# Graph attention with a mixture of experts on one core: reordered normalisation, scanned bf16 ranks, a bf16 table of slots ahead of the shared outputs, and a fourth buffer for edge keys

## The chip, the cores and the metric

The kernel runs on 1 core of one Trainium2 chip. The metric is the device time of one execution in microseconds (us); lower is better. A core has five engines with queues of their own: PE (TensorE, matmuls), DVE (VectorE), ACT (ScalarE), POOL (GpSimd, which here gathers and scatters rows by indirect DMA) and SP (SyncE, which issues most transfers). They meet only at semaphores: `wait_ge` holds up the engine's whole queue, `then_inc` signals at the end of an instruction.

## The reference, cut to what matters

1250 tokens of 512 numbers, 20000 edges sorted by destination, 64 experts.

```
x = x + gnn(layernorm(x))                 # graph attention, 8 heads of 64
   h = x @ W.T;  e = leaky_relu(e_src[src] + e_dst[dst]) * (1 + et_emb[type]) * weight
   alpha = softmax of e over the edges of one dst
   out = layernorm(sum over edges of h[src] * alpha + x) * ln_gamma + ln_beta
x = x + ffn(layernorm(x))
   scores = sigmoid(x @ Wg.T + bg);  w, idx = top 2 of 64, w normalised
   y = sum over the two experts of w * (silu(h1) * h3) @ W2 + b2   # own gamma, beta, W1, W3 per expert
   z = shared expert: (silu(nxs @ Ws1 + bs1) * (nxs @ Ws3 + bs3)) @ Ws2 + bs2
   result x + y + z
```

## The kernel before

All numbers of the tokens live in SBUF as NT = 10 tiles of 128 rows. The program is written out by hand, one block for each engine, and the order of each queue is the order of the code. Its stages, in order of time:

**Selection of attention terms.** Per edge and head, `e_src[src]` and `e_dst[dst]` are picked by matmuls with one-hot matrices. The keys (src mod 128, dst mod 128, type) lie in DRAM as `edge_keys`. 160 chunks of 128 edges make 16 pieces of 10 chunks, each read in two groups of 5 (32 groups). For a piece SP loads three key rows, broadcast over the partitions, into one of three buffers (`keys[q % 3]`, L414); it waits until PE has done piece q-3. DVE makes one-hots of src and type (`hot`, L1241 and L1243), ACT those of dst (`hot_dst`, L659 and L661), PE multiplies (L920, L925), DVE picks (L1340) and sums (L1289). Both `hot(q + 2)` and `hot_dst(q + 2)` stand in their queues ahead of the last group of piece q. After each odd group up to 19 PE also computes one tile of h (L901), ACT copies it out and SP stores it (`HELD`, L419) behind the keys of piece t+3. Once all ten are stored, POOL starts its 176 gathers of h rows (L569).

**Softmax and items.** DVE scans, then 88 items of two gathered chunks each are scaled by DVE and ACT, summed by PE (L969) and added by DVE (L1445). POOL's gathers reuse 23 pairs of buffers, so gather 46 waits for the first item.

**Normalisation and router.** The tiles go in five steps of two (`LNG`). DVE: `gnn_sum` (statistics, L1491 and L1494), `x1_sum` (L1505 to L1515), `x1_scale` (L1520 to L1522, which waits for ACT's square roots), `best_two` (logits and top 2, L1529 to L1537). ACT: `root` (L715), `x1_spread` (L721 to L725), `x1_normalise` (L731, and L735, the copies of the transposed tiles). PE: four transposes a tile (L825) and four logit matmuls (L994). The order of DVE is

```
                if 0 <= step - 2 < G:
                    x1_scale(step - 2)
                if step < G:
                    gnn_sum(step)
                if 0 <= step - 1 < G:
                    x1_sum(step - 1)
```

**Ranks and slots.** From the top 2 DVE makes one-hots over experts (`oh`), their sum `hits`, and the running sum over tiles `before` (ten dependent adds, L1597). PE turns these into ranks within each expert by matmuls with a triangle and with ones (f32, L1030 to L1032). A chain of some 25 DVE instructions (L1601 to L1633) makes the slot of each token. Then `rank1h` (L1637) and `tile1h` (L1639, times `payload` L1641) are multiplied on PE (20 f32 matmuls of 72 columns, L1042) into the table of slots, of which DVE makes indices (L1648 to L1652) and POOL the first two gathers of tokens (L594).

**Shared expert beside it.** `shared_up(k)` (L1008) is two halves of four f32 matmuls of 512 columns each (gate and up), `shared_gate` its silu on ACT (L753), `shared_hidden` the product on DVE (L1549); `shared_down(t)` (L1014) and `shared_add` (L1542) give tile t. `sil` is one buffer, so gate k waits for hidden k-1. PE's order is up(0), ranks, up(1), up(2), down(0), down(1), table of slots, up(3), turn of the first tokens, down(2), then the pair loop, in which the rest of the shared work is spread by `BESIDE` (`aside`).

**Pair loop.** 32 pairs of experts and one overflow expert, NJ = 33 steps. Step j: `up` (L1071, L1075), the turn of the next tokens (L825), `down` of step j-1 (L1088), `aside(j)`, `hidden_turn`. Weights lie in three buffers; SP loads the 2 MB of up weights of step j+3 when PE has done up of step j (L445), ACT the 1 MB of down weights after `down` (L777). At the end POOL has scattered the expert rows to `y_rows`, and SP, DVE and ACT bring them back, add and store them tile by tile.

## Time and profile before

| what | us |
|---|---|
| median of 3 runs (lowest, highest) | 751.66 (750.05, 753.65) |
| the profiled execution | 749.77 |
| its span | 748.0 |
| busy in the span: PE, DVE, ACT, POOL | 612.7, 486.6, 234.5, 263.0 |

The profiled execution's time is 1.8 us above its span; the span is what the engines' rows cover, and all rows shown here count from its start. The stages lie about like this in it: selection 42 to 149, softmax 149 to 181, items 181 to 356, normalisation and router 356 to 405, ranks and slots with the first shared work 405 to 448, pair loop 448 to 718, the end to 748. A stretch's row gives each engine's busy time with the number of instructions, then the clock granted to PE as a share of 2.4 GHz, the busy share of the DMA engines and what they moved.

### The profile page before, as it was taken

The page shows a single profiled execution, that of the slowest core. Times are in us where ns is not written, and L with a number is a line of the kernel's source. Part 1 is how long each engine was busy: PE and PEld are TensorE (multiplying, and loading weights), DVE is VectorE, ACT ScalarE, POOL GpSimd, SP SyncE. Part 2 cuts the span into 40 slices and gives each one's busy share as a digit, 9 for nine tenths or more (in the row PEclk, how much of TensorE's full clock was granted, in tenths as well). Part 3 has the DMA queues.
Part 4 walks back from the last instruction along what each step waited for, and adds up shares of the span by engine and source line. Part 5 has one row for each costly group of instructions (what it writes and reads, how often), then busy time and mean ns, then how long its engine had stood idle before and what let it go on. Part 6 is the DMA issues. An engine that isn't in the chain of part 4 may idle for free. (4 is left out here: it accounts for less than half of the span.)

```text
span 748.0 us, 9448 instructions
## 1 busy us (share of the span) xinstructions
PE 612.7 (82%) x3091; PEld 297.1 (40%) x3091; DVE 486.6 (65%) x950; ACT 234.5 (31%) x575; POOL 263.0 (35%) x281
## 2 busy tenths in 40 slices
PE   2979996534999999999089999999999999998940
PEld 2645665522333333333077453443333333332310
DVE  5886778897999999998777745533233333332307
ACT  1563554514755443435276210111111111111110
POOL 3000005775777777778400011222222222222210
PEclk9898998655999999999655999999999999998985
DMA  8433667866779977795721007999999999999929
GB/s 258 122 82 100 158 157 240 252 182 174 209 211 336 361 227 211 212 371 177 273 85 56 1 19 276 397 379 409 414 414 412 409 414 411 380 379 414 364 79 364
DMA packets 68135, 194.30 MB, mean 260 GB/s; under 512 B 14539, under 2 KB 15621, under 8 KB 68086
## 3 DMA queue, kind: packets, MB, share of 16 engines
q1 hardware_dynamic: 37270, 100.70, 37.2%
q0 software_dynamic: 19600, 56.41, 23.9%
q10 hardware_dynamic: 11216, 36.58, 12.6%
q8 instruction: 25, 0.41, 0.2%
q14 instruction: 24, 0.20, 0.1%
HBM read 184.31 MB, written 16.58 MB: 269 GB/s over the span
## 5 line engine op out<-in xcount | busy, mean ns | idle before, releaser
L599 POOL DMA_INDIRECT y_rows<-nxb,slot_tab x33 | 34.3, 1040 | 193.1 <-ACT nxb L784 191.2
L1711 DVE TENSOR_TENSOR nxb<-ps,nxb 128x256 f32<-128x256 f32 (+1 forms) x33 | 14.0, 424 | 134.3 <-PE ps L1075 73.1
L569 POOL DMA_INDIRECT nxb<-h_rows,srcx x50 | 47.5, 951 | 128.8 <-DMA h_rows<-ring 108.9
L1075 PE MATMUL ps<-arena,nxb 128*64 128x512 f32 x352 | 82.1, 609 | 0.0
L569 POOL DMA_INDIRECT ring<-h_rows,srcx x74 | 71.0, 960 | 23.5 <-issue 20.7
L969 PE MATMUL ps<-ring,edge 128*128 128x512 f32 x148 | 67.3, 603 | 7.4 <-issue 6.8
L825 PE MATMUL ps<-ident,nxb 128*128 128x128 f32 (+1 forms) x248 | 49.5, 321 | 20.3 <-ACT nxb L731 19.7
L825 PEld LDWEIGHTS ps<-ident,nxb 128*128 128x128 f32 (+1 forms) x248 | 39.2, 207 | 65.2 <-issue 57.7
L1088 PE MATMUL ps<-arena,nxb 128*64 128x512 f32 x260 | 63.9, 604 | 0.9 <-DVE nxb L1714 0.9
L1445 DVE TENSOR_TENSOR xn<-ps,xn 128x512 f32 x88 | 60.9, 692 | 2.4 <-PE ps L969 1.5
L781 ACT ACTIVATE nxb<-ps 128x256 f32<-128x256 f32 (+1 forms) x33 | 12.7, 384 | 155.5 <-PE ps L1075 155.5
L707 ACT ACTIVATE ring<-ring,edge 128x64 f32<-128x64 f32 x148 | 37.7, 335 | 58.0 <-DVEq L1434 39.5
L969 PE MATMUL ps<-nxb,edge 128*128 128x512 f32 x100 | 46.4, 615 | 6.0 <-ACT nxb L707 4.2
L784 ACT COPY nxb<-ps 128x512 f32<-128x512 f32 (+1 forms) x33 | 19.3, 585 | 83.4 <-PE ps L1088 83.4
L969 PEld LDWEIGHTS ps<-ring,edge 128*128 128x128 f32 x148 | 26.2, 189 | 47.4 <-issue 47.4
L1340 DVE TENSOR_TENSOR x_sb<-ps,arena 128x400 f32<-128x400 f32 x64 | 33.5, 562 | 17.4 <-PE ps L925 16.5
L569 POOL DMA_INDIRECT xT<-h_rows,srcx x42 | 40.1, 954 | 12.8 <-issue 11.3
L1075 PE MATMUL ps<-edge,nxb 128*64 128x512 f32 x168 | 42.8, 632 | 0.0
L901 PE MATMUL ps<-arena,xT 128*128 128x512 f32 x80 | 40.0, 645 | 3.4 <-DVE dloc L1281 3.4
L594 POOL DMA_INDIRECT nxb<-nx_rows,slot_tab x34 | 34.7, 1020 | 20.2 <-issue 10.7
L1075 PEld LDWEIGHTS ps<-arena,nxb 128*64 128x64 f32 x352 | 23.7, 138 | 45.3 <-issue 45.3
L969 PE MATMUL ps<-xT,edge 128*128 128x512 f32 x84 | 37.9, 601 | 2.1 <-issue 1.8
(300 smaller groups left out, 1047.0 us busy)
## 6 DMA issues: line engine op xcount, KB each, us to landing
arena<-in_L_ffn_W_dram SPq DMA_DIRECT2D x47, 1024.0 KB, 12.4
arena<-in_L_ffn_W_dram ACTq DMA_DIRECT2D x29, 1024.0 KB, 10.4
edge<-in_L_ffn_W_dram SPq DMA_DIRECT2D x20, 1024.0 KB, 12.6
arena<-edge_keys SPq DMA_DIRECT2D x22, 320.0 KB
ring<-y_rows SPq DMA_DIRECT2D x9, 512.0 KB, 6.9
ring<-edge_keys SPq DMA_DIRECT2D x10, 320.0 KB
h_rows<-ring SPq DMA_DIRECT2D x10, 256.0 KB, 2.0
nx_rows<-nxb SPq DMA_DIRECT2D x10, 256.0 KB, 2.0
```

What stands on the lines that cost most here:

```text
L569: pool.indirect_dma_start(out=slot(k), out_offset=None, in_=h_d[:, :], in_offset=bass.IndirectOffsetOnAxis(ap=srcx[:, k:k + 1], axis=0)).t ...
L594: pool.indirect_dma_start(out=xg[:, u, :], out_offset=None, in_=nx_d[:, :], in_offset=bass.IndirectOffsetOnAxis(ap=at, axis=0), bounds_che ...
L599: pool.indirect_dma_start(out=y_d[:, :], out_offset=bass.IndirectOffsetOnAxis(ap=at, axis=0), in_=yo[:, u, :], in_offset=None, bounds_chec ...
L707: o = act.activation(slot(k)[:, h * HD:(h + 1) * HD], slot(k)[:, h * HD:(h + 1) * HD], ACT.Copy, scale=p_c[:, k, h:h + 1])
L784: act.copy(yo[0:rows, k, :], ps[0:rows, 5 + k, :]).then_inc(s(done), 1)
L825: return pe.transpose(o, i, ident[0:n, 0:n])
L901: o = pe.matmul(ps[:, 7, :], xT[:, a, t * P:(t + 1) * P], WT[:, a, :], start=(a == 0), stop=(a == A - 1))
L969: o = pe.matmul(ps[:, BANKS[i % len(BANKS)], :], S[:, k % (2 * SB), :], slot(k), start=(u == 0), stop=(u == 1))
L1075: o = pe.matmul(ps[c, 2 + k, :], xgT[:, k, a, c], w13[b][:, x, :, a, :], start=False, stop=(a == A - 1), skip_group_check=True)
L1088: o = pe.matmul(ps[c, 5 + k, :], hT[:, k, m, c], w2s[b][:, x, m, :], start=(m == 0), stop=(m == M - 1))
L1340: v.tensor_tensor(pr[:, side, :, :, :], ps[:, 2 * (g % 2) + side, 0:n * NT * H].rearrange("p (c h a) -> p c h a", c=n, a=NT), sel_hi[:, si ...
L1445: v.tensor_tensor(a, ps[:, BANKS[i % len(BANKS)], :], a, ALU.add).then_inc(s("acc_done"), 1)
```

## The change

1. **Fourth key buffer.** `keys` gets a fourth buffer in tiles 4 to 7 of `x_sb`, free once the first layer norm is done; `% 3` becomes `% 4`, SP waits for piece q-4, and the stores of h stand behind the keys of piece t+4, with the same waits in front of them.
2. **Order of normalisation.** On DVE `gnn_sum(step)` comes ahead of `x1_scale(step - 2)`. `rank_masks` (casts of the triangle and of ones, and two memsets) is added ahead of `bias_high`.
3. **Ranks.** `hits` is written expert-major in bf16; one scan over 640 elements, reset at every expert by a mask, replaces the ten adds; the rank matmuls are bf16 (480 and 160 columns) and come after only the first half of up(0).
4. **Slots.** The one-hots are bf16. The payload is split: position and side within a tile, which bf16 holds exactly, in `tile_lo` on DVE, and 256 t in `tile_hi`, nine small activations on ACT. 20 + 18 bf16 matmuls sum both in one bank. They come ahead of down(0) and down(1). DVE runs `shared_hidden(0)` after the chain of slots and `shared_hidden(1)` after the one-hots.
5. **Banks and order of the shared work.** up(k) gets banks of its own in PSUM with fewer waits; only half of up(3) stays ahead of the loop, the other half goes into step 0 (`BESIDE`).

```diff
@@ keys and their loads
+        keys.append(Carver(x_sb[:, 4:8, :].rearrange("p t d -> p (t d)"), 4 * D)([P, 3, PIECE * P], BF16))
-            HELD[min(GROUPS[g][0] + 3, len(PIECES) - 1)].append(t)
+            HELD[min(GROUPS[g][0] + 4, len(PIECES) - 1)].append(t)
-                if q >= 3:
-                    sp.wait_ge(s("pe_sel"), sum(1 for g in GROUPS if g[0] <= q - 3))
+                if q == 3:
+                    sp.wait_ge(s("ln1"), NT)
+                if q >= 4:
+                    sp.wait_ge(s("pe_sel"), sum(1 for g in GROUPS if g[0] <= q - 4))
...
@@ banks and spread of the shared work
+    BESIDE = {0: (("half", 3),), 2: (("up", 4),), ...
+    UP_BANKS = ((4, 5), (1, 2), (4, 5), (3, 5), (1, 7), (1, 7))
+    UP_FREE = ((0, 0), (0, 0), (1, 1), (0, 3), (4, 4), (5, 5))
...
@@ ACT, ahead of gates 2 and 3
+                    if n == 1:
+                        act.wait_ge(s("route_step"), 2)
+                        for t in range(1, NT):
+                            o = act.activation(tile_hi[:, 2 * t:2 * t + 2, :], tile1h[:, 2 * t:2 * t + 2, :], ACT.Identity,
+                                               scale=2.0 * P * t)
+                        o.then_inc(s("act_route"), 1)
@@ PE
-            shared_up(0)
-            pe.wait_ge(s("before_done"), 1)
-            for t0, t1 in ((0, 8), (8, NT)):
...
+            shared_half(0, 0)
+            pe.wait_ge(s("lg_read"), NT)
+            pe.wait_ge(s("route_step"), 1)
+            for n, (e0, e1) in enumerate(RANKS):
+                o = ps[:, 6 + n, 0:(e1 - e0) * NT]
+                pe.matmul(o, tri_b[:, :], hits[:, e0:e1, :].rearrange("p e t -> p (e t)"), start=True, stop=False)
+                pe.matmul(o, ones_b[:, :], upto[:, e0:e1, :].rearrange("p e t -> p (e t)"), start=False, stop=True)
+            pe.matmul(ps[:, 7, 3 * NEX:4 * NEX], ones_b[:, :], upto[:, :, NT - 1], start=True, stop=True).then_inc(s("pe_rank"), 1)
+            shared_half(0, 1)
             shared_up(1)
             shared_up(2)
-            pe.wait_ge(s("lg_read"), NT)
+            pe.wait_ge(s("route_step"), 3)
+            for k in range(2 * NT):
+                pe.matmul(ps[:, 0, 0:NCOL], rank1h[:, k, :], tile_lo[:, k, :], start=(k == 0), stop=False)
+            pe.wait_ge(s("act_route"), 1)
+            for k in range(2, 2 * NT):
+                o = pe.matmul(ps[:, 0, 0:NCOL], rank1h[:, k, :], tile_hi[:, k, :], start=False, stop=(k == 2 * NT - 1))
+            o.then_inc(s("pe_slots"), 1)
             pe.wait_ge(s("hs_done"), M)
             shared_down(0, SPARE[1])
             shared_down(1, SPARE[0])
-            pe.wait_ge(s("onehots"), 1)
-            for k in range(2 * NT):
-                o = pe.matmul(ps[:, 0, 0:NCOL], rank1h[:, k, :], tile1h[:, k, :], start=(k == 0), stop=(k == 2 * NT - 1))
-            o.then_inc(s("pe_slots"), 1)
-            shared_up(3)
+            shared_half(3, 0)
...
@@ DVE
+            def rank_masks():
+                v.wait_ge(s("tri_done"), 5)
+                v.tensor_scalar(tri_b[:, :], tri[:, :], -1.0, None, ALU.add)
+                v.tensor_copy(ones_b[:, :], ones[:, :])
+                link(v.memset(within[:, :, :], 1.0))
+                v.memset(within[:, :, 0:1], 0.0)
...
+                if step < G:
+                    gnn_sum(step)
                 if 0 <= step - 2 < G:
                     x1_scale(step - 2)
-                if step < G:
-                    gnn_sum(step)
...
-            for t in range(NT):
-                link(v.tensor_tensor(before[:, t + 1, :], before[:, t, :], hits[:, t, :], ALU.add))
-            v.nop().then_inc(s("before_done"), 1)
-            shared_hidden(0)
+            link(v.tensor_tensor_scan(upto.rearrange("p e t -> p (e t)"), within.rearrange("p e t -> p (e t)"),
+                                      hits.rearrange("p e t -> p (e t)"), 0.0, ALU.mult, ALU.add))
+            v.nop().then_inc(s("route_step"), 1)
...
-            shared_hidden(1)
+            shared_hidden(0)
...
+            v.tensor_copy(iota_b[:, :], iota_row[:, :])
+            v.tensor_copy(pay_b[:, :], payload[:, :, :].rearrange("p t k -> p (t k)"))
+            v.tensor_copy(rank_b[:, :], rf)
+            link(v.tensor_copy(tile_b[:, :], of))
+            link(v.tensor_tensor(tile1h[:, :, :], iota_b[:, 0:NCOL].unsqueeze(1).to_broadcast([P, 2 * NT, NCOL]),
+                                 tile_b[:, :].unsqueeze(2).to_broadcast([P, 2 * NT, NCOL]), ALU.is_equal))
+            v.nop().then_inc(s("route_step"), 1)
+            v.tensor_tensor(rank1h[:, :, :], iota_b[:, :].unsqueeze(1).to_broadcast([P, 2 * NT, P]),
+                            rank_b[:, :].unsqueeze(2).to_broadcast([P, 2 * NT, P]), ALU.is_equal)
+            v.tensor_tensor(tile_lo[:, :, :], tile1h[:, :, :], pay_b[:, :].unsqueeze(2).to_broadcast([P, 2 * NT, NCOL]),
+                            ALU.mult).then_inc(s("route_step"), 1)
+            shared_hidden(1)
```

`shared_half(k, w)` is the inner part of the old `shared_up` for one of its two weights, with its bank and its wait from the two tables above.

## Rows read from the trace of the kernel before

**Rows 1.** The page's slices of the span: DMA engines busy, in tenths.
```profile
DMA  8433667866779977795721007999999999999929
```
**Rows 2.** Stretches: PE, PEld, DVE, ACT, POOL busy (instructions), PE clock, DMA share, GB/s.
```profile
75.00:100.00 25.00, 25.00 (x312) 16.39 (x311) 18.66 (x33) 13.23 (x12) 0.00 (x0) 1.00 0.62 157
...
455.00:460.00 5.00, 4.95 (x23) 1.91 (x25) 0.74 (x3) 0.38 (x1) 0.00 (x0) 1.00 0.95 386
```
**Rows 3.** Timeline of SP's queue: start, length, line, transfers issued.
```profile
126.14 1.59 SPq L414 DMA_DIRECT2D arena<-edge_keys  x3
...
452.52 7.42 SPq L445 DMA_DIRECT2D arena<-in_L_ffn_W_dram  x4
```
**Rows 4.** Timeline of DVE, end of the selection; in brackets the idle time before.
```profile
128.92 0.55 DVE L1241 TENSOR_SCALAR ring<-ring,iota_p 128x1280 bf16<-128x1280 bf16 x1 [1.43 <-DMA ring<-edge_keys]
...
135.37 0.55 DVE L1241 TENSOR_SCALAR arena<-arena,iota_p 128x1280 bf16<-128x1280 bf16 x1 [1.53 <-DMA arena<-edge_keys]
```
**Rows 5.** Timeline of POOL, the gather that waits for the first item.
```profile
185.83 0.94 POOL L569 DMA_INDIRECT nxb<-h_rows,srcx  x1 [5.31 <-PE ps L969]
```
**Rows 6.** Timeline of DVE, one step of the normalisation.
```profile
373.73 0.18 DVE L1520 RECIPROCAL rv<-vw 128x4 f32<-128x4 f32 x1 [2.10 <-ACT vw L725]
...
374.09 1.28 DVE L1491 BATCH_NORM_STATS2 stats<-xn 128x6 f32<-128x512 f32 x2
...
375.56 1.38 DVE L1505 SCALAR_TENSOR_TENSOR xn<-xn,mv,arena 128x512 f32<-128x512 f32 x2
...
378.52 0.17 DVE L1515 TENSOR_SCALAR sums<-sums 128x2 f32<-128x2 f32 x1
```
**Rows 7.** Timeline of ACT: one step of the normalisation, and four small scalings.
```profile
371.66 0.72 ACT L721 ACTIVATE nxb<-x_sb,sums 128x512 f32<-128x512 f32 x1 [2.75 <-DVE sums L1515]
...
373.60 1.50 ACT L731 ACTIVATE nxb<-x_sb,mean,rv 128x512 f32<-128x512 f32 x2
...
377.01 0.30 ACT L715 ACTIVATE rstd<-mv,eps 128x2 f32<-128x2 f32 x1
...
330.96 1.06 ACT L707 ACTIVATE nxb<-nxb,edge 128x64 f32<-128x64 f32 x4 [1.72 <-DMA nxb<-h_rows,srcx]
```
**Rows 8.** The chain that ended last: start, length, engine and line.
```profile
394.21 1.98 PE ps L825 x8
396.19 3.50 PE ps L994 x16
...
404.98 9.74 PE ps L1008 x16
...
417.10 1.22 DVE xn L1601
...
426.83 0.76 DVE ring L1549
...
427.64 3.70 PE ps L1008 x8
...
434.77 4.42 PE ps L1042 x40
...
446.11 0.47 PE ps L825 x4
...
453.99 1.06 issue
```
**Rows 9.** A stretch of half a microsecond in which PE's clock rises (columns as in rows 2).
```profile
410.00:410.50 0.50, 0.50 (x2) 0.23 (x1) 0.43 (x3) 0.00 (x0) 0.00 (x0) 0.70 0.00 0
```
**Rows 10.** DVE groups by shape: busy us, mean ns of one.
```profile
L1371 DVE TENSOR_TENSOR_SCAN arena<-arena 128x1280 f32<-128x1280 bf16 x2 | 5.7, 2825 | 0.1
...
L1637 DVE TENSOR_TENSOR nxb<-iota_row,rnk 128x2560 f32<-128x2560 f32 x1 | 2.8, 2817 | 0.0
...
L1641 DVE TENSOR_TENSOR nxb<-nxb,payload 128x1440 f32<-128x1440 f32 x1 | 1.7, 1657 | 0.0
```
**Rows 11.** Timeline of PE, one group's 30 bf16 matmuls of 80 columns.
```profile
82.92 1.25 PE L920 MATMUL ps<-arena,ring 128*128 128x80 bf16 x30
```

More of the change, by code:

```diff
@@ L326, in gnn_moe_kernel @@
         onehots = Carver(nxb[:, :, :].rearrange("p t d -> p (t d)"), NT * D)
-        rank1h = onehots([P, 2 * NT, P])
-        tile1h = onehots([P, 2 * NT, NCOL])
+        rank1h = onehots([P, 2 * NT, P], BF16)
+        tile1h = onehots([P, 2 * NT, NCOL], BF16)
+        tile_lo = onehots([P, 2 * NT, NCOL], BF16)
+        tile_hi = onehots([P, 2 * NT, NCOL], BF16)
+        iota_b = onehots([P, P], BF16)
+        rank_b = onehots([P, 2 * NT], BF16)
+        tile_b = onehots([P, 2 * NT], BF16)
+        pay_b = onehots([P, 2 * NT], BF16)
         lg = router([P, NT, NEX])
@@ L332, in gnn_moe_kernel @@
         tmp = router([P, NT, 2, NEX])
-        hits = router([P, NT, NEX])
-        before = router([P, NT + 1, NEX])
+        hits = router([P, NEX, NT], BF16)
+        upto = router([P, NEX, NT], BF16)
+        within = router([P, NEX, NT], BF16)
+        tri_b = router([P, P], BF16)
+        ones_b = router([P, P], BF16)
         eidx = sb("eidx", [P, NT, 2])
@@ L363, in gnn_moe_kernel @@
         y_out = [sem(f"y_out{k}") for k in range(2)]
-        rows_in = [sem(f"rows_in{k}") for k in range(7)]
+        rows_in = [sem(f"rows_in{k}") for k in range(8)]
         landed = [sem(f"row_landed{k}") for k in range(len(AGAIN))]
@@ L376, in gnn_moe_kernel @@
         KP = NE // 160
-        KEY_ROWS = [48 * len(PIECES[k::3]) for k in range(3)]
+        KEY_ROWS = [48 * len(PIECES[k::4]) for k in range(4)]
         H_AT = {2 * t + 1: t for t in range(NT)}
@@ L1003, in shared_up @@
                 pe.wait_ge(s("nxs_done"), A * (n + 1))
-                for w, read in ((0, "act_sh"), (1, "hs_done")):
-                    if k:
-                        pe.wait_ge(s(read), k)
-                    for a in range(A):
-                        o = pe.matmul(ps[:, 4 + w if k < 4 else SPARE[w], 0:c], ws13[:, w, a, m * P:(m + 1) * P],
-                                      xT[:, a, c0:c1], start=(a == 0), stop=(a == A - 1))
-                    o.then_inc(s("pe_sh1" if w == 0 else "pe_sh3"), 1)
+                if UP_FREE[k][w]:
+                    pe.wait_ge(s(("act_sh", "hs_done")[w]), UP_FREE[k][w])
+                for a in range(A):
+                    o = pe.matmul(ps[:, UP_BANKS[k][w], 0:c], ws13[:, w, a, m * P:(m + 1) * P],
+                                  xT[:, a, c0:c1], start=(a == 0), stop=(a == A - 1))
+                o.then_inc(s("pe_sh1" if w == 0 else "pe_sh3"), 1)
+            def shared_up(k):
+                shared_half(k, 0)
+                shared_half(k, 1)
             def shared_down(t, bank):
@@ L1038, in _ @@
             shared_down(1, SPARE[0])
-            pe.wait_ge(s("onehots"), 1)
-            for k in range(2 * NT):
-                o = pe.matmul(ps[:, 0, 0:NCOL], rank1h[:, k, :], tile1h[:, k, :], start=(k == 0), stop=(k == 2 * NT - 1))
-            o.then_inc(s("pe_slots"), 1)
-            shared_up(3)
+            shared_half(3, 0)
             def aside(j):
-                for name, count in (("zh_added", DOWN0 + beside(j, "down")), ("hs_done", 4 + beside(j, "up")),
+                for name, count in (("zh_added", DOWN0 + beside(j, "down")), ("hs_done", 3 + beside(j, "half") + beside(j, "up")),
                                     ("cwT_done", beside(j, "cw"))):
@@ L1054, in aside @@
                         shared_up(k)
+                    elif kind == "half":
+                        shared_half(k, 1)
                     elif kind == "down":
@@ L1578, in _ @@
                 if step - 4 == G - 2:
+                    rank_masks()
                     bias_high()
@@ L1740, in _ @@
                 for n, (kind, k) in enumerate(BESIDE.get(j, ())):
-                    if kind == "up":
+                    if kind in ("up", "half"):
                         shared_hidden(k)
```

71 lines of the change are left out of this document (31 added, 40 removed).

## The prediction, made before the changed kernel was run

> **What bounds the kernel now.** I read the page's slices first, then stretches, then the chain that ended last, and last the timelines of single engines. In the slices the DMA digits are to be looked at: ones to nines until the items end, zeros in the two slices from 411 to 449, and nearly unbroken nines from the 26th slice on, until the weights are through [rows 1]. The stretch that starts at 455 has the DMA engines 0.95 busy with 386 GB/s [rows 2]. So from 455 to about 705 the kernel is a stream of expert weights of about 250 us. SP issues its first load when PE has done `up` of step 0, at 452.52 [rows 3]. The chain of waits goes over PE from 448 to 559 and then over the transfers; both are nearly full until there. What is saved inside the loop is worth little. What brings 452.52 forward moves the whole stream, as long as it stays full.
>
> Ahead of that point are three stages with other limits. (a) Selection: while PE also computes the ten tiles of h, PE is the bound (25.00 of 25.00 us busy between 75 and 100 [rows 2]); a key buffer gives nothing there. Behind the tiles DVE is the bound and stands still only where keys are late: 1.43 and 1.53 us [rows 4]. (b) Items: POOL issues gathers back to back but for one wait of 5.31 us for the first item's buffer, which releases it at 185.8 [rows 5]. (c) From 356 to 448: DVE and ACT in turns, then PE, as worked out below.
>
> **Fourth key buffer.** Keys of piece 15 are issued at 126.14 and come into use at 135.37, 9.2 us later [rows 3, 4]; POOL's gathers run beside them. DVE stands at them because the load waits for PE at piece 12, two pieces before DVE asks for it. With four buffers each load goes out one piece earlier, some 5 us in this tail, against waits of 1.5 us each. Even if the whole 2.96 us by which DVE gets ahead is counted against the second load, 5 - 2.96 = 2.0 us of margin exceed its 1.53. Both waits go: 1.43 + 1.53 = 2.96 us. PE can feed the faster pace: even at its lower clock a group takes some 2.5 us there, and DVE asks for two groups in 5.1. The loads still number 48, so SP issues nothing more; the stores of h keep their place in time, since both waits in front of them are the same. The wait for the first layer norm holds only SP's fourth load, and nobody waits for that one before the selection.
> Do the 2.96 us survive the items? POOL is the faster limit there, but it first waits 5.31 us for DVE [rows 5]. If DVE comes 2.96 earlier, 2.35 us of the wait remain, and everything behind it shifts by 2.96. Bounds: 0 (keys are late all the same, or POOL is the bound) to 3. I take 2.9.
>
> **Normalisation.** One step of DVE before: wait 2.10 us for ACT, `x1_scale` 373.73 to 374.09, `gnn_sum` to 375.56, `x1_sum` to about 378.6; ACT's spread starts at 371.66 and releases DVE at 373.7 [rows 6, 7]. The period is 378.73 - 371.66, 7.07 us. In the new order `gnn_sum`, 1.47 us, fills the wait of 2.10, so DVE and the spread alone would turn in 7.07 - 1.47 = 5.6 us. ACT needs 371.66 to 377.31 for spread, normalising, copies and `root`: 5.65 [rows 7]. PE needs 1.98 + 3.50 and a start, 5.6 us, at 1.2 GHz, the clock that the whole stretch is granted [rows 8]. The three come out equal, so the period becomes about 5.7. Before, the two steps between PE's first three turns (374.5, 381.5, 388.6) took 7.0 each and the last two, PE-bound, 5.6 each. PE's first turn comes 1.2 earlier (a step ahead of it is only half relieved, `params_by_row` lies there), the two slow steps give 1.3 each: 1.2 + 2.6 = 3.8 us. `rank_masks` is four small instructions, under 1 us together, and stands where DVE waits 1.2 us for PE: free; on the path it would cost that 1 us. Bounds: 1.5 (ACT's order adds a wait) to 4.5. I take 3.8.
>
> **Ranks.** In the time of before: PE starts up(0) at 404.98 and ends at 414.73 [rows 8]; the clock rises at 410.3 [rows 9], so the first half ends at 411.3. One scan of 640 elements replaces ten adds of 2.56 us together; 1280 elements take 2.83 us [rows 10], so it takes 1.4 to 1.5 (if bf16 output costs the double, 2.8, it is no later than now). DVE is then ready at 410.4 to 411.5, PE at 411.3. The rank matmuls took 2.4 us in f32; bf16 needs one pass for 1344 columns: 30 matmuls of 80 columns take 1.25 us [rows 11], so 0.6 to 1.0. DVE starts the chain at 412.2 instead of 417.10 [rows 8]: 4.9 us earlier. The chain itself, 417.10 to 426.83, 9.73 us [rows 8], is the same but for the strided operands from PSUM, whose cost I bound by 0 and 1.6 us (twice the two products) and take at 0, as other rows with rearranged PSUM operands run at one element a cycle. It ends at 421.9.
>
> **Slots.** DVE then runs hidden(0) 0.7, four copies 0.6, and the three one-hot instructions. In f32 these take 1.65, 2.82 and 1.66 us [rows 10]. The three end at 429.3 at those prices and at 426.2 if bf16 halves them. I take 429.3.
> The Trainium skill, VectorE: DVE Perf Modes, section on the tier table, gives a tensor_tensor in bf16 twice the f32 rate, and the section on what auto-detection checks wants step 1 for every tensor, which the operand spread over the innermost axis has not. By the first sentence the sum would not move by more than 0.2 us, since PE is not free before 429.1; no row here has an all-bf16 tensor_tensor.
> PE in the meantime: after the ranks (412.1) it has five halves. A half is 3.43 us at 2.4 GHz (8 instructions in 3.70 with their start [rows 8]): 429.3. DVE and PE arrive together. The 20 + 18 bf16 matmuls of 72 columns cost 38 x 0.042 = 1.6 us [rows 11] against 4.42 [rows 8]. `tile_hi`: nine activations of 144 elements; four of 64 take 1.06, two of 512 take 1.50 [rows 7], so 2.4 to 6.8 us for nine. ACT starts them at 425.4, behind gate 1 (422.7) and the 2.07 us of the last `shared_in`; they are wanted at 430.1. At 0.32 each they end at 428.4 and cost nothing; at the upper end they cost 2 us, and gates 2 and 3 queue behind them, which nobody wants before 430.9. The table is done at 430.9 instead of 439.19: 8.3 us.
> Then DVE makes indices (1.0), POOL gathers (ready within 4.4 us of them, as PE found its rows without a wait at 446.11): 436.4. PE does down(0), down(1) and half of up(3), 3 x 3.43 = 10.3, to 438.0 plus 0.2 for handing over: it is the later one. First turn at 438.0 instead of 446.11 [rows 8], so `up` of step 0 ends 8.1 us earlier, at 444.4 against 452.52 [rows 3].
>
> **The loop.** The moved half, 3.43 us, stands in step 0 between the turn of the next tokens and `hidden_turn`. PE had about 0.5 and 1.06 us of waits there [rows 8], which it covers; the rest, 1.9, is new. From step 1 on PE is 8.1 - 1.9 = 6.2 us early. For the weight stream: load 3 goes out at 444.4 and is through by about 452, load 4 goes out at 452.8 (459.0 before). From there every load is issued 6.2 us earlier than before and the stream has a little less in hand, up to 1 us. It ends 6.2 to 7.2 us earlier. I take 6.5. The banks and counts that `UP_FREE` changes let PE start earlier or equally; hidden(3) comes 8 us before down of step 0 overwrites its bank.
>
> **Sum.** 2.9 + 3.8 + 6.5 = 13.2 us. The profiled execution, 749.77, would become 736.6. It lies 1.9 under the median of 751.66, so the median becomes 738.4.
>
> **Rivals.**
> *The selection gives nothing.* POOL's stream, not DVE, sets the items' end, or the keys collide with gathers. For it: POOL does not stop after the first item for more than 1.3 us. Against it: the 5.31 us [rows 5]. Time 738.4 + 2.9 = 741.3.
> *The clock rises earlier.* PE is at 1.2 GHz from 356 on and rises only 5.3 us into the 512-column matmuls [rows 8, 9], although it is busy without a break from 388.6. The new order makes it busy from 373 on. If that brings the rise ahead of 405, PE's last steps and half(0, 0) shrink, until DVE with its 3.6 us of `bias_low` is the bound: up to 3 us more. Against it: 16 us of full busy at these small shapes, 388.6 to 405, did not raise it. Time 735.5.
> The Trainium skill, TensorE: Matmul & The Clock Gate, says that activity releases the throttle; by its wording alone a denser stretch speaks for this rival, the trace's 16 us speak against it.
> *Slower: the clock does not rise in time.* The first half is followed by a wait or by the short bf16 ranks, where 512-column work followed without a break. If PE stays at 1.2 GHz, each half or down tile pair costs 3.4 us more. There are eight such blocks from the ranks to the first pair. It decides from four blocks on (4 x 3.4 = 13.6, the whole gain); with all eight, 738.4 + 27 = 765.8. Against it: the rise came while the same first half ran, and it does so again.
> *The loop takes it back.* The moved half leaves the DMA engines idle for some 2 us after load 3, and a later wait in the early steps (gates against hidden 3) repeats it. The gain of the last part falls from 6.5 to 3: 741.9.
> *ACT becomes the bound.* `tile_hi` or ACT's step of the normalisation lies on the path, 2 us each at most: 740 to 742.
>
> **How the numbers follow.** Forecast 0.57 (735 to 741); selection nothing 0.10; loop or ACT takes 2 to 4 us 0.13; clock earlier 0.13; clock late 0.04, half of it slower than before; something small that I do not see, within 4 us of before, 0.03. The range 733.5 to 743.5 holds the main case, the bounds of the unknown costs and most of the three near rivals. Half a per cent of the time, 3.8 us, is about what a measurement of this kernel tells from no change. All cases but the last two lie more than that under 751.66: faster 0.94, same 0.03, slower 0.03.
>
> **What would show it.** Selection: DVE's key waits near 128 and 135 gone, the last sum near 146; POOL's wait about 2.4 us. Normalisation: PE's turns 5.7 us apart, `x1_scale` without 2.10 us in front. Ranks: DVE's chain starting about 7 us after up(0) starts instead of 12. Slots: table done 18 to 19 us after the rank matmuls, PE without a wait over 0.5 us there. Loop: SP's first load near 437.7 in the span (452.52 - 2.9 - 3.8 - 8.1), the second 8.4 us behind it instead of 6.5, and the weights through near 699. Wrong: a clock of 0.5 beyond the first half; ACT as releaser of PE at the table; DMA below 0.9 busy in the first 20 us of the loop.

## The result and the profile after

The changed kernel takes 737.94 us (median of 6 runs, 736.99 to 739.57), the kernel before 750.41 in the same comparison (748.88 to 753.65): ratio 0.9831, 95% interval 0.9808 to 0.9854. The forecast was 738.4. The profiled execution took 737.98 with a span of 736.2, against 748.0 of the span before.

The whole is told best by stages. Each begins and ends at a row that both timelines have: the last pick of DVE at the pace of the h tiles, the last sum of the selection, the first normalising `scalar_tensor_tensor` of the stage behind the items, the start of up(0), the end of the table of slots, load 3 (SP's first in the loop), the first read of y, the end of the span.

| stage, us | before | after | gain |
|---|---|---|---|
| start to last pick at the tiles' pace | 108.23 | 106.87 | 1.36 |
| selection to its last sum | 38.44 | 35.36 | 3.08 |
| items, to the first normalising | 212.45 | 213.45 | -1.00 |
| normalisation, to up(0) | 45.86 | 41.62 | 4.24 |
| routing, to the table of slots | 34.21 | 25.80 | 8.41 |
| to load 3 | 13.33 | 13.02 | 0.31 |
| load 3 to the first read of y | 273.01 | 276.42 | -3.41 |
| last reads, sums and stores | 22.47 | 23.66 | -1.19 |
| sum | 748.0 | 736.2 | 11.8 |

The rows of after that answer to those of before follow. First PE's timeline from up(0) to the up of step 1 (columns: start, duration, engine, line, operation and tiles, count, and in brackets the idle time before it with what ended it):

```profile
397.30 5.42 PE L1028 MATMUL ps<-xT,ring 128*128 128x512 f32 x8
403.67 0.36 PE L1055 MATMUL ps<-xn 128*128 128x480 bf16 x1 [0.95 <-DVEq L1635]
...
404.31 17.35 PE L1028 MATMUL ps<-xT,ring 128*128 128x512 f32 x40
421.70 0.82 PE L1064 MATMUL ps<-nxb 128*128 128x72 bf16 x20
...
422.94 3.68 PE L1038 MATMUL ps<-ring 128*128 128x512 f32 x8
426.45 3.60 PE L1028 MATMUL ps<-xT,ring 128*128 128x512 f32 x8
...
432.42 3.66 PE L1105 MATMUL ps<-arena,nxb 128*64 128x512 f32 x16
...
436.59 3.60 PE L1028 MATMUL ps<-xT,ring 128*128 128x512 f32 x8
...
440.57 3.65 PE L1105 MATMUL ps<-arena,nxb 128*64 128x512 f32 x16
```

up(0) starts 7.68 us earlier [rows 8]. Its first half takes 5.42: the clock comes up between 400 and 401 (granted 0.59 in this microsecond, 0.50 before it, 1.00 behind), some 3.5 us into it. Then PE waits 0.95 us, the only wait up to the loop that is new. L1064 is the new table; the two shared outputs (L1038) and half of up(3) (L1028) stand behind it, and at 436.59 the other half stands in step 0. SP's loads and the read of y, the same columns; the first row holds two loads, load 3 at 436.12 and load 4 at 444.26:

```profile
436.12 9.03 SPq L460 DMA_DIRECT2D arena<-in_L_ffn_W_dram  x4
451.05 0.96 SPq L460 DMA_DIRECT2D edge<-in_L_ffn_W_dram  x2
...
712.54 9.00 SPq L535 DMA_DIRECT2D ring<-y_rows  x10
```

DVE on its way from `hits` to the one-hots, and its waits in the normalisation [rows 6]:

```profile
374.57 0.18 DVE L1550 RECIPROCAL rv<-vw 128x4 f32<-128x4 f32 x1 [0.63 <-ACT vw L740]
...
400.37 1.58 DVE L1632 TENSOR_TENSOR xn<-xn 128x640 bf16<-128x640 f32 x1
401.98 1.49 DVE L1633 TENSOR_TENSOR_SCAN xn<-xn 128x640 bf16<-128x640 bf16 x1
404.53 1.15 DVE L1639 TENSOR_TENSOR xn<-xn,ps 128x960 f32<-128x960 f32 x1 [1.06 <-PE ps L1057]
...
414.27 0.75 DVE L1579 SCALAR_TENSOR_TENSOR ring<-ps,arena,ring 128x512 f32<-128x512 f32 x1
...
415.43 1.66 DVE L1680 TENSOR_TENSOR nxb<-nxb 128x1440 bf16<-128x1440 bf16 x1
417.24 2.83 DVE L1683 TENSOR_TENSOR nxb<-nxb 128x2560 bf16<-128x2560 bf16 x1 [0.16 <-DVE nxb L1680]
```

The wait of 2.10 us for ACT is down to 0.63. The chain starts at 404.53, 12.6 us earlier, and hidden(0) at 414.27 ends it 9.74 us later: as long as before. The one-hots in bf16 take 1.66 and 2.83 us, within 0.02 us of the float32 prices of [rows 10]. ACT's timeline with `tile_hi`:

```profile
417.67 2.01 ACT L790 ACTIVATE nxb<-nxb 128x144 bf16<-128x144 bf16 x9
```

POOL's timeline, with its wait for the first item [rows 5]:

```profile
181.74 0.94 POOL L584 DMA_INDIRECT nxb<-h_rows,srcx  x1 [3.21 <-PE ps L990]
...
220.93 0.94 POOL L584 DMA_INDIRECT ring<-h_rows,srcx  x1 [1.98 <-PE ps L990]
```

The second row is POOL's next long wait in the items, thirty gathers on. In the kernel before it is shorter:

```profile
224.43 0.94 POOL L569 DMA_INDIRECT ring<-h_rows,srcx  x1 [1.29 <-PE ps L969]
```

### The profile page after: what moved, and what is told of

The parts are those of the page before. It is cut to its first block and busy times, and to the rows that moved or that the text cites. A ratio compares the mean times of both kernels' runs of the same rounds, so it can differ in the third digit from the quotient of the medians.

```text
span 736.2 us, 9445 instructions
## 1 busy us (share of the span) xinstructions
PE 607.2 (82%) x3084; PEld 295.8 (40%) x3084; DVE 487.8 (66%) x948; ACT 235.6 (32%) x584; POOL 262.1 (36%) x281
## 5 line engine op out<-in xcount | busy, mean ns | idle before, releaser
L1105 PE MATMUL ps<-arena,nxb 128*64 128x512 f32 x352 | 80.4, 599 | 0.0
L1118 PE MATMUL ps<-arena,nxb 128*64 128x512 f32 x260 | 63.9, 605 | 0.9 <-DVE nxb L1758 0.9
L584 POOL DMA_INDIRECT xT<-h_rows,srcx x42 | 41.7, 992 | 12.8 <-issue 11.9
L922 PE MATMUL ps<-arena,xT 128*128 128x512 f32 x80 | 37.7, 615 | 2.1 <-DVE dloc L1311 2.1
## 6 DMA issues: line engine op xcount, KB each, us to landing
arena<-in_L_ffn_W_dram SPq DMA_DIRECT2D x47, 1024.0 KB, 12.6
arena<-in_L_ffn_W_dram ACTq DMA_DIRECT2D x29, 1024.0 KB, 10.3
```

The source lines that it names most:

```text
L584: pool.indirect_dma_start(out=slot(k), out_offset=None, in_=h_d[:, :], in_offset=bass.IndirectOffsetOnAxis(ap=srcx[:, k:k + 1], axis=0)).t ...
L922: o = pe.matmul(ps[:, 7, :], xT[:, a, t * P:(t + 1) * P], WT[:, a, :], start=(a == 0), stop=(a == A - 1))
L1105: o = pe.matmul(ps[c, 2 + k, :], xgT[:, k, a, c], w13[b][:, x, :, a, :], start=False, stop=(a == A - 1), skip_group_check=True)
L1118: o = pe.matmul(ps[c, 5 + k, :], hT[:, k, m, c], w2s[b][:, x, m, :], start=(m == 0), stop=(m == M - 1))
```

## The experiments

Medians of one kernel differ between chips by more than a part of the change is worth, and the 95% intervals of the ratios reach 0.2 to 0.5 per cent to either side. So each verdict below is taken from the stages of the profiled execution. In the profiles up to e8, versions that share a stage have selection within 0.4 us, normalisation and routing within 0.5, load 3 to the read of y within 1.6, the last stage within 1.5. (e9 to e12 ran on a slower chip and have a paragraph of their own.) The start, up to the last pick at the tiles' pace, scatters from 106.4 to 109.7 us among versions that are equal up to there, so its gain of 1.36 is within chance; e1, with three key buffers as before, starts like the changed kernel (107.01). "Ratio" is to the kernel before, run beside each version.

**e1: three key buffers again.**

```
-        keys.append(Carver(x_sb[:, 4:8, :]...)([P, 3, PIECE * P], BF16))
-                if q >= 4:
-                    sp.wait_ge(s("pe_sel"), sum(1 for g in GROUPS if g[0] <= q - 4))
+                if q >= 3:
+                    sp.wait_ge(s("pe_sel"), sum(1 for g in GROUPS if g[0] <= q - 3))
...
```

> The changed kernel with three key buffers again, all else kept. Theory (a buffer takes away only the two DVE waits for keys): the waits of about 1.4 and 1.5 us come back near 127 and 133 us, the items end about 3 us later (355 instead of 352.0), POOL's wait for the first item grows again to over 4.5 us, and the time is 741 (738 + 3.0). Rival (POOL's gathers set the end of the items, the buffer's gain is swallowed there): 738, with POOL's wait grown and the items ending at 352 all the same.

Median 741.15, ratio 0.9852 (0.9818 to 0.9886). DVE's timeline of this version:

```profile
121.64 0.55 DVE L1268 TENSOR_SCALAR arena<-arena,iota_p 128x1280 bf16<-128x1280 bf16 x1 [0.69 <-DMA arena<-edge_keys]
...
128.80 0.78 DVE L1268 TENSOR_SCALAR ring<-ring,iota_p 128x1280 bf16<-128x1280 bf16 x1 [2.24 <-DMA ring<-edge_keys]
...
135.09 0.74 DVE L1268 TENSOR_SCALAR arena<-arena,iota_p 128x1280 bf16<-128x1280 bf16 x1 [1.09 <-DMA arena<-edge_keys]
```

Three waits, 4.02 us, are back, the selection takes 39.62 instead of 35.36, POOL's wait grows from 3.21 to 6.96, and at the start of the normalisation 3.8 us are left. The theory holds, the rival falls. Some of the gain does stay in the items: the two profiles with three buffers have 212.5 and 213.0 us there, those with four 213.3 to 214.3. In the changed kernel 2.1 of its 3.08 arrived: POOL's release came 4.09 us earlier where DVE's last sum came 4.44 earlier, which leaves 0.35 open, and POOL's second wait took another 0.7 (1.98 us instead of 1.29).

**e2: the old order of a normalisation step.**

```
+                if 0 <= step - 2 < G:
+                    x1_scale(step - 2)
                 if step < G:
                     gnn_sum(step)
-                if 0 <= step - 2 < G:
-                    x1_scale(step - 2)
```

> The changed kernel with the old order in a step of the normalisation (x1_scale, then gnn_sum), all else kept. Theory (the wait of DVE for ACT's spread, 2.10 us, was on the path in the steps before PE is full): the wait comes back, PE's first turns are 7.0 us apart, up(0) starts 3.8 to 4.3 us later (401.1 to 401.6 instead of 397.3), time 742. Rival (the earlier start of up(0) came from the clock of early stretches and from the selection): up(0) at 398 to 399, time 738.5 to 739.5.

Median 743.05, ratio 0.9863 (0.9826 to 0.99). The wait is back in DVE's timeline:

```profile
373.29 0.18 DVE L1550 RECIPROCAL rv<-vw 128x4 f32<-128x4 f32 x1 [2.10 <-ACT vw L740]
```

The stage takes 45.94 us against 41.62 (before: 45.86), 4.3 us. up(0) starts at 404.56, later than expected, because the start of this execution was 2.6 us slower and its items 0.4; the stage is free of both. The theory holds.

**e3: half of up(3) in step 1.**

```
-    BESIDE = {0: (("half", 3),), 2: (("up", 4),), ...
-    UP_BANKS = ((4, 5), (1, 2), (4, 5), (3, 5), (1, 7), (1, 7))
+    BESIDE = {1: (("half", 3),), 2: (("up", 4),), ...
+    UP_BANKS = ((4, 5), (1, 2), (4, 5), (3, 1), (1, 7), (1, 7))
...
```

> The moved half of up(3) runs in step 1 of the loop instead of step 0. In the changed kernel the DMA engines stand idle for about 2 us (443.2 to 445.2) between the weights of load 3 and those of load 4, which waits for up of step 1. Theory A (this gap is what the stream lost): up of step 1 ends at 440.6 instead of 444.2, the gap closes, the weights are through 2 us earlier, time 736. Theory B (the weights' end is set by other things, and the 1.8 us lost between step 1 and the last weights are scatter of the DMA rate): load 4 goes out 3.6 us earlier, but the last weights land when they did, 738.

Median 741.41, ratio 0.9835 (0.9791 to 0.9879). PE's timeline:

```profile
434.43 3.65 PE L1105 MATMUL ps<-arena,nxb 128*64 128x512 f32 x16
...
440.66 0.38 PE L1101 MATMUL ps<-arena,nxb 96*128 96x512 bf16 x1 [1.06 <-issue]
440.97 5.35 PE L1105 MATMUL ps<-arena,nxb 128*64 128x512 f32 x16
```

The up of step 1 came only 1.6 us earlier behind that of step 0 (6.54 instead of 8.14), as the half had covered two waits of 0.33 and 1.06 us, and then took 5.35 us instead of 3.65. So load 4 went out 8.24 us behind load 3, no earlier than in the changed kernel (8.14), and 7.5 to 10 us behind load 3 the DMA engines were 0.29 busy: the gap did not close. Load 5, now behind the half, went out 18.4 us behind load 3 instead of 14.9. Load 3 to the read of y: 277.5. The earlier load 4, which both theories assume, did not happen, so this run doesn't decide between them; it shows that the half, moved on by a step, delays the next load instead.

**e4: hits written strided.**

```
-  v.tensor_tensor(hits[:, :, :], oh[:, :, 0, :].rearrange("p t e -> p e t"), oh[:, :, 1, :].rearrange(...), ALU.add)
+  v.tensor_tensor(hits.rearrange("p e t -> p t e"), oh[:, :, 0, :], oh[:, :, 1, :], ALU.add)
```

> The sum that makes hits reads its two operands in their own order and writes strided, where it read strided and wrote contiguous (1.58 us instead of the 0.76 that was assumed; PE waited 0.95 us for it). Theory (strided reads cost the double, a strided write doesn't): the instruction takes 0.76 to 0.8 us, PE's wait ahead of the rank matmuls shrinks to under 0.2 us, time 737.2 (0.8 less). Rival (any strided operand costs the double): 1.6 us again, and 738.0.

Median 739.97, ratio 0.9829 (0.9794 to 0.9864). DVE's timeline:

```profile
399.64 3.02 DVE L1632 TENSOR_TENSOR xn<-xn 128x640 bf16<-128x640 f32 x1
```

Neither: with the strided write of bf16 the instruction takes 3.02 us, about twice its time with strided reads (1.58), and the table comes 1.2 us later (26.96). The changed kernel has the cheaper of the two.

**e5: half of up(3) in step 2.**

```
-    BESIDE = {0: (("half", 3),), 2: (("up", 4),), 3: (("cw", 0), ("cw", 1)), 4: (("up", 5),), 5: (("cw", 2),), ...
+    BESIDE = {2: (("half", 3),), 3: (("up", 4),), 4: (("cw", 0), ("cw", 1)), 5: (("up", 5),), ... 9: (("cw", 2),), ...
...
```

> The moved half of up(3) runs in step 2 of the loop; up(4) goes from step 2 to 3, the transposes of the weights from 3 to 4, up(5) from 4 to 5, the last transpose from 5 to 9. Nothing stands beside the up of steps 0 and 1 any more. In four profiles of the changed kernel and its variants, first load to start of the last phase takes 275.8 to 276.9 us, before 273.0. Theory (what was lost is the DMA engines' gap between loads 3 and 4, which any work put ahead of up of step 1 or 2 opens): loads 4 and 5 go out 6.5 and 13.3 us after load 3, as before, the gap (now a stretch of 0.35 busy, 7.5 to 10 us behind load 3) closes, load 3 to last phase is 273 to 274.5, and the time is 2 to 3 us under the changed kernel's (ratio to before about 0.980). Rival (the loss lies behind load 5, in the steps that follow): the gap closes and the last phase starts 276 us behind load 3 all the same.

Median 740.83, ratio 0.9837 (0.9801 to 0.9872). Loads 4 and 5 went out 8.24 and 15.02 us behind load 3, not 6.5 and 13.3 as expected, and the gap did not close. SP's timeline (the row holds loads 3 and 4):

```profile
439.39 9.12 SPq L460 DMA_DIRECT2D arena<-in_L_ffn_W_dram  x4
```

PE's timeline:

```profile
440.37 0.50 PE L846 MATMUL ps<-ident,nxb 128*128 128x128 f32 x2 [0.33 <-DVE nxb L1755]
441.93 0.38 PE L1101 MATMUL ps<-arena,nxb 96*128 96x512 bf16 x1 [1.06 <-issue]
442.24 5.35 PE L1105 MATMUL ps<-arena,nxb 128*64 128x512 f32 x16
```

Two stretches of it (columns: length, PE busy and count, granted clock, DMA share, GB/s):

```profile
442.30:444.80 2.50, 2.50 (x7) 0.50 1.02 416
...
446.80:449.30 2.50, 2.50 (x14) 1.00 0.41 48
```

Behind the waits of 0.33 and 1.06 us the granted clock is 0.50, the level of 1.2 GHz, and the up of step 1 takes 1.70 us longer, as in e3. Load 3 to the read of y stays at 277.1. The experiment doesn't tell its theories apart: the fall of the clock, a second effect, held load 4 back.

**e6: both halves ahead of the loop.**

```
-    BESIDE = {0: (("half", 3),), 2: ...
+    BESIDE = {2: ...
...
             shared_half(3, 0)
+            shared_half(3, 1)
...
```

> Both halves of up(3) run ahead of the loop, nothing in step 0: the old place. Theory: the first turn and load 3 come 3.6 us later (first up of the table to load 3 18.0 instead of 14.4 us), loads 4 and 5 are 6.5 and 13.3 us behind it, load 3 to last phase falls from 276.4 to about 273.5, so that of the 3.6 us of the move 0.5 to 2 are net, and the time is 0.5 to 2 us over the changed kernel's. Rival (load 3's time counts in full): load 3 to last phase stays 276 and the time rises by 3.6.

Median 741.95, ratio 0.9848 (0.9804 to 0.9891). PE's timeline:

```profile
429.44 7.03 PE L1028 MATMUL ps<-xT,ring 128*128 128x512 f32 x16
...
443.86 0.51 PE L846 MATMUL ps<-ident,nxb 128*128 128x128 f32 x2 [0.33 <-DVE nxb L1757]
445.42 0.38 PE L1102 MATMUL ps<-arena,nxb 96*128 96x512 bf16 x1 [1.06 <-issue]
445.73 3.65 PE L1106 MATMUL ps<-arena,nxb 128*64 128x512 f32 x16
```

SP's loads of the same execution:

```profile
442.88 7.42 SPq L460 DMA_DIRECT2D arena<-in_L_ffn_W_dram  x4
456.21 0.98 SPq L460 DMA_DIRECT2D edge<-in_L_ffn_W_dram  x2
```

Load 3 comes 3.77 us later behind the table (16.79 against 13.02), and load 3 to the read of y is 3.56 shorter (272.86 against 276.42). The two cancel within the scatter, where I had expected 0.5 to 2 us of the move to remain: the part of the change that takes this half out of the way of load 3 gains nothing that shows. The stretch 7.5 to 10 us behind load 3, in before, after and here, shows the gap that load 4 leaves (columns as in e5). Before:

```profile
460.02:462.52 2.50, 2.50 (x13) 1.00 0.98 269
```

After:

```profile
443.62:446.12 2.50, 2.50 (x14) 1.00 0.36 48
```

This version:

```profile
450.38:452.88 2.50, 2.50 (x13) 1.00 0.90 292
```

The DMA engines are 0.98, 0.36 and 0.90 busy. The same two waits as in e3 and e5 stand here too, and the clock held: the up of step 1 took 3.65.

**e7: the table in float32.**

```
-        rank1h = onehots([P, 2 * NT, P], BF16)
-        tile1h = onehots([P, 2 * NT, NCOL], BF16)
-        tile_lo, tile_hi, iota_b, rank_b, tile_b, pay_b = ...
+        rank1h = onehots([P, 2 * NT, P])
+        tile1h = onehots([P, 2 * NT, NCOL])
...
```

> The table of slots from float32 one-hots again, in one group of 20 matmul pairs' time (4.42 us before, 1.41 changed), without tile_hi and the four copies; it still stands ahead of the shared outputs. Theory: PE is the bound there, so the table is done 3.0 us later, first load 3.0 us later, time 3 us over the changed kernel's. DVE's three one-hot instructions take 1.65, 2.83 and 1.66 in bf16, as in float32, so DVE loses nothing. Rival (the gathers, not PE, decide the first turn, since two shared outputs and a half stand behind the table): first load at most 1 us later.

Median 741.7, ratio 0.9862 (0.983 to 0.9895). The table in PE's timeline:

```profile
422.84 4.58 PE L1052 MATMUL ps<-nxb 128*128 128x72 f32 x40
```

The table is done 2.95 us later (28.75), load 3 follows 12.98 behind it, the loop is 276.3: the whole comes through. The theory holds.

**e8: the shared outputs ahead of the table.**

```
+            pe.wait_ge(s("hs_done"), M)
+            shared_down(0, SPARE[1])
+            shared_down(1, SPARE[0])
             pe.wait_ge(s("route_step"), 3)
...
```

> down(0) and down(1) ahead of the table again (3.68 us of PE), all else kept. Theory: the table is done 3.6 us later; the indices and the gathers take some 6 us behind it, half(3, 0) covers 3.6 of them, PE then waits some 2.5 us, so the first turn is 2.5 to 3.6 us later and the time 2.5 to 3.6 us over the changed kernel's. Rival (order is free, PE has the same work before the first turn): no wait, first turn within 0.5 us.

Median 741.86, ratio 0.9866 (0.9833 to 0.99). PE's timeline:

```profile
422.70 3.70 PE L1038 MATMUL ps<-ring 128*128 128x512 f32 x8 [0.69 <-DVE ring L1579]
...
433.01 0.75 PE L846 MATMUL ps<-ident,nxb 128*128 128x128 f32 x4 [1.86 <-DMA nxb<-nx_rows,slot_tab]
```

The table is done 4.17 later (29.97; 0.69 of it is a wait for hidden(0)), PE then stands 1.86 us for the gathered rows, and load 3 is 11.72 behind the table: 2.87 in all, as expected.

Together e7 and e8 return 7.1 of the 8.4 us that the routing stage gained up to the table. The other 1.3 falls to the new ranks (scan, bf16 matmuls, their place behind half of up(0)); no run undoes these by themselves, nor the new banks of the shared work.

**e9: down(0) and down(1) in steps 13 and 14.** This came from e6: if PE's work between the table and the up of step 2 sets the stream, wherever in it a piece stands, there has to be less of it.

```
-    BESIDE = {0: (("half", 3),), 2: ... 14: (("down", 9),)}
-    DOWN0 = 3
+    BESIDE = {2: ... 13: (("down", 0),), 14: (("down", 9), ("down", 1))}
+    DOWN0 = 1
...
-            shared_down(0, SPARE[1])
-            shared_down(1, SPARE[0])
             shared_half(3, 0)
+            shared_half(3, 1)
...
```

> Both halves of up(3) stand behind the table, ahead of the loop, in the place of down(0) and down(1), which run in steps 13 and 14 of the loop. Nothing is beside up of steps 0 and 1. Theory (PE's work between the table and up of step 2 sets the whole stream, wherever in it a piece stands; it is 3.6 us less here): load 3 goes out 13.0 us behind the table as in the changed kernel, loads 4 and 5 6.5 and 13.3 us behind it, load 3 to last phase 273, time 3.4 us under the changed kernel's. If PE's clock falls to half behind the two short waits of step 0 (0.33 and 1.06 us), as in two of the four profiles that had them, up of step 1 takes 5.35 instead of 3.65 and the gain is 1.7. Rival (PE is as full in the later steps, the two downs cost there what they saved here): no gain.

**e10: as e9, with down(0) in step 0.**

```
+    BESIDE = {0: (("down", 0),), 2: ... 13: (("down", 1),), 14: (("down", 9),)}
...
```

> As the version with down(0) and down(1) in steps 13 and 14, but down(0), 1.9 us of PE, stands in step 0 and fills the two short waits there; down(1) runs in step 13. Theory: up of step 1 comes 7.1 us behind up of step 0 (6.54 with the waits, 8.14 with half(3, 1)), no wait over 0.2 us stands ahead of it and the clock stays at full; time 2.5 to 3 us under the changed kernel's. Rival (the waits of step 0 are latency of hm and of the turn, which no filling shortens, and the clock would have held anyway): 0.5 us slower than with the downs in 13 and 14.

**e11: the changed kernel beside them.**

> The changed kernel once more, on the chip of the two versions beside it. If its stages are as fixed as the variants suggest: 35.3 us from DVE's last pick at the pace of the h tiles to the last sum, 41.6 from the first normalising to up(0), 25.8 to the end of the table, 13.0 to load 3, 14.9 from load 3 to load 5, 276.4 to the last phase, each within 0.5 us; the start of the selection scatters by up to 3 us. Against it: if the loss of 3.4 us behind load 3 was chance, load 3 to last phase comes out at 273 to 275.

These three ran on a chip on which all versions, the kernel before too (834.47 us), are 11 to 12% slower. Medians 824.73, 821.07 and 826.36; ratios 0.9863 (0.9813 to 0.9914), 0.9834 (0.9802 to 0.9865) and 0.9901 (0.987 to 0.9932). The excess lies ahead of up(0): in e11 it starts at 486.66 instead of 397.30, and from there the span has 337.2 us (338.9 in the first profile of this kernel). By the last sum of the selection e11 is 35.4 us late, and the items add 56.2 (269.7 against 213.5). In the selection ACT stands for keys that land late, and DVE in the same stretch for something that the profile does not name ("remote"). Waits of e11 between 110 and 170 (engine, tile and line, what was waited for: us, times, longest):

```profile
DVE x_sb L1370 <- remote: 34.3, 3, 24.9
...
ACT x_sb L674 <- DMA x_sb<-edge_keys: 13.7, 1, 13.7
```

The normalisation, from the first normalising instruction to up(0), takes 39.4 us in all four of these profiles, 2.2 less than in the first profile of the changed kernel. The difference lies in its first two instructions on DVE. In the first profile they run beside the last additions of beta on POOL:

```profile
354.40 3.69 POOL L591 TENSOR_TENSOR x_sb<-x_sb,arena 128x512 f32<-128x512 f32 x3
...
355.68 3.62 DVE L1535 SCALAR_TENSOR_TENSOR xn<-xn,mv,arena 128x512 f32<-128x512 f32 x2
```

In e11 POOL has long been done:

```profile
447.28 1.38 DVE L1535 SCALAR_TENSOR_TENSOR xn<-xn,mv,arena 128x512 f32<-128x512 f32 x2
```

The first of the two instructions takes 2.7 to 3.1 us in all ten profiles in which POOL adds beside it, the kernel before among them, and 0.7 in the four in which it doesn't. No run moves POOL's additions, so the cause is read from this alone. The 2.2 us are in before and after alike and no part of the gain.

Of the stages that I had expected of e11, table, load 3 and load 5 came as named (25.8, 13.0, 14.9); selection and normalisation did not, and load 3 to the read of y is 0.8 off. Behind up(0) the stages can be compared:

| us | e11 | e9 | e10 | e12 |
|---|---|---|---|---|
| end of table to load 3 | 13.02 | 13.36 | 13.36 | 13.36 |
| load 3 to load 5 | 14.93 | 13.32 | 13.32 | 13.33 |
| load 3 to the read of y | 275.64 | 273.99 | 272.44 | 272.19 |
| up(0) to the end | 337.24 | 336.15 | 334.84 | 334.52 |

The loss behind load 3 is no chance: seven profiles with half of up(3) in step 0 have 275.3 to 276.9, five with at most a shared output there, before among them, 272.2 to 274.0. PE's timeline in step 0 of e10:

```profile
519.90 3.65 PE L1104 MATMUL ps<-arena,nxb 128*64 128x512 f32 x16
...
524.08 1.88 PE L1039 MATMUL ps<-ring 128*128 128x512 f32 x4
...
526.44 3.65 PE L1104 MATMUL ps<-arena,nxb 128*64 128x512 f32 x16
```

The stretch 7.5 to 10 us behind its load 3:

```profile
531.10:533.60 2.50, 2.50 (x13) 1.00 0.95 301
```

down(0) costs nothing there: the up of step 1 begins 6.54 us behind that of step 0, as with the two waits. I had expected 7.1. Whether it also guards the clock these runs don't show, since the clock held in e9 too. Against e11 e9 gains 1.1 us from up(0) on, e10 2.4. For e9 I had expected 3.4, and that was too much: of the 3.6 us of work that are gone ahead of the up of step 2, the half in step 0 had already put 2.0 into time that stood empty, so load 5 comes only 1.6 us earlier behind load 3 (13.32 against 14.93), and load 3 itself 0.3 later behind the table. With profiles that share a loop up to 1.6 us apart in it, e9's gain is not clear of its rival; e10's is helped by the fact that e12 repeats it.

**e12: e10 once more.**

> The same version as before it (both halves of up(3) ahead of the loop, down(0) in step 0, down(1) in step 13), now to be seen on a chip without the long waits for transfers in the selection. Theory: stages as there, 13.3 us from the end of the table to load 3, 13.3 from load 3 to load 5, 272.4 to 273.5 to the last phase, where the changed kernel has 13.0, 14.9 and 276.4: 3 us less than the changed kernel in all, ratio to before 0.979 against 0.983. Rival (the gain of 5 us on the slow chip was chance or belongs to that chip): ratio 0.983 and 276 to the last phase.

It fell on the same slow chip, so the question of another chip stays open. Median 822.82, ratio 0.9848 (0.9804 to 0.9893), not the 0.979 that I had named for another chip, where the changed kernel had 0.9831; here that one has 0.9901. The stages repeat e10's. From up(0) on it takes 334.5 us, where four profiles of kernels with the changed routing and loop (after, e1, e2, e11) have 337.2 to 338.9: 2.7 to 4.4 less. By stages it is the best version of the case; by medians, 3.5 to 5.3 us under e11's, and the interval of e12's ratio overlaps that of e11's.

## Why the prediction was right

The time was met to 0.5 us. The mechanisms of selection, normalisation and routing were right; the loop was mis-sized. Part of the closeness is luck. The forecast gain was 13.2 us; the medians of the same comparison are 12.5 apart and the spans 11.8. By terms, 2.9 + 3.8 + 6.5 were forecast and 2.1 + 4.2 + 5.3 = 11.6 came, and the scatter of the first stage (1.36) and the last (-1.19) cancels. The profiled execution was forecast at 736.6 and took 737.98; the forecast median stood 1.9 above it, and the measured one stands level with it.

*Selection.* Both waits went (38.44 to 35.36, 3.08 against the 2.96 forecast), and e1 shows the cause. Of this 2.1 reached the normalisation; I took 2.9, as if everything behind POOL's first wait moved with it. POOL's second wait grew by 0.7 us instead, which I had not looked at. The margin of the first wait stood: 3.21 us were left, more than the forecast 2.4. The reason is POOL, which I had held fixed: it reached this gather 1.99 us earlier while the release came 4.09 us earlier. The early start is not the reason, for the wait is 3.21 or 3.22 in all eight profiles with four buffers up to e8, whose starts lie 3.3 us apart.

*Normalisation.* Forecast 3.8, measured 4.24, and 4.3 by e2. PE's turns are 5.5 to 5.6 us apart where the three engines turn together, against 5.7 forecast.

*Ranks.* The chain was to start 7 us behind up(0); it started at 7.23. Inside, two things cancelled: the clock rose 3.5 us into the first half instead of 5.3, and `hits`, to which I gave no more than it cost before, took 1.58 us; its operands are now read across the one-hots. This term was mis-sized by 0.8, most of PE's wait of 0.95. The row of before:

```profile
408.12 0.76 DVE L1595 TENSOR_TENSOR xn<-xn 128x640 f32<-128x640 f32 x1
```

The strided operands from PSUM, bounded by 0 and 1.6 us, cost nothing that shows: the chain took 9.74 us.

*Slots.* The table was done 18.6 us behind the ranks (18 to 19 forecast), the routing stage gave 8.4 us where 8.3 were forecast, and the one-hots stood at the float32 prices that I had chosen. The Trainium skill, VectorE: DVE Perf Modes, section What auto-detection actually checks, wants 16-bit elements with step 1 in every tensor for the double rate of a tensor_tensor. The broadcast operand has no such step, and the trace's 1.66 and 2.83 us agree. `tile_hi` took 0.22 us each, below the 0.32 taken, well off the path. One line of my working was wrong though its time was right: from the table to the first turn I wrote three blocks of 3.43 us, 10.3 in all, but the time of 438.0 behind 430.9 holds two. Two shared outputs are one block (8 matmuls in 3.68), the half is the other (3.60).

*Slower or faster clock.* The clock did not rise ahead of up(0): it was granted at 0.50 (1.2 GHz) though PE had no wait over 0.14 us from 369.8 on. Nor did it stay low. (In before it fell between 359 and 360, not at 356 as I wrote; nothing hangs on that.)

*The loop.* This is the step that failed: "From there every load is issued 6.2 us earlier than before and the stream has a little less in hand", up to 1 us of it lost. I set 6.5 us, with 1.9 of the 8.1 lost to the later load 4 and up to 1 in the stream; the same sum measured is 8.72 - 3.41 = 5.31 us. The moved half delays loads 4 and 5 against load 3 by 1.6 us: of its 3.6, the two waits of 0.33 and 1.06 take up 1.4, and 0.6 goes where no row shows a wait. The DMA engines have finished load 3 by then and idle (0.36 busy). I had named a DMA share below 0.9 in the first 20 us as a sign of error, and it came (0.85, against 0.93 before). That the half in step 0 is the price is shown by e6, where it is gone, the gap with it, and the stream is 3.56 us shorter. Of these 3.4 to 3.6 us the delay of load 5, 14.93 - 13.32 = 1.6 us, is one part. The rest is not explained by a row: at 20 us behind load 3 the stream is 0.5 MB, some 1.3 us, behind, and at 200 us 1.0 MB. The rival "the loop takes it back" came to a third: of the 3.5 us by which it cut this term, 1.2 came, and no later step repeated the gap as it had it.

*The last stage* took 1.2 us more than before. The profiles have 22.5 to 23.9 there in all versions, so I count it as scatter.

## What to carry to other kernels

When work is moved out of the way of the first transfer of a stream, ask which transfer it now stands in front of. Here half of up(3) cost the stream as much behind load 3 as it had cost load 3 (e6), and moved on by one or two steps it was no cheaper (e3, e5, both under a fall of the clock). Work that leaves the first steps for much later ones, with a short piece in waits that stand there anyway, gave 2.4 us from up(0) on and more (e10, e12), on one chip. Compare stages between rows that both timelines have; medians alone would have told apart almost none of these versions.

## What the hardware showed that was not expected

- A `tensor_tensor` of 640 elements with float32 inputs takes 0.76 us with runs of 64 elements read and float32 written, 1.58 us when both inputs are read at a stride of 512 bytes and bf16 is written in order, 3.02 us when they are read in runs and bf16 is written at a stride of 20 bytes.
- A DVE `scalar_tensor_tensor` of 512 elements took 2.7 to 3.1 us beside POOL's `tensor_tensor` and 0.7 us without it, in ten and four profiles.
- After PE idled 0.33 and 1.06 us in step 0, the granted clock went to 0.50 in two of five profiles with these waits (e3, e5) and cost 1.70 us; in before, e6 and e9 it stayed at 1.00.
- One chip ran the kernel before and the changed one 84 and 88 us slower; in the changed one all of it lies ahead of up(0), 35 us by the end of the selection, where ACT waited 13.7 us for keys and DVE up to 24.9 us at a time, and 56 us in the items. Why was not tried.
